# The expert loop of a mixture-of-experts tail: two expert numbers per register load, no runtime assert

## What is computed

```python
logits = jnp.einsum('bsh,eh->bse', x, router_w)
rw = jax.nn.softmax(logits, axis=-1).reshape(T, E)
vals, idx = jax.lax.top_k(rw, TOP_K)          # TOP_K = 2
w_masked = jnp.zeros_like(rw).at[jnp.arange(T)[:, None], idx].set(vals)
# out = sum over experts e of (x_flat * w_masked[:, e]) @ expert_weights[e]
x = x + out
```

## Time and profile before

| what | us |
|---|---|
| median of 3 executions | 2840.68 |
| lowest, highest | 2838.80, 2844.18 |
| profiled execution: span from first to last instruction | 2781.7 |
| median less span | 59.0 |

### The profile page before, as it was taken

One profiled execution on the slowest core, in us unless ns is written; L12 is line 12 of the kernel. 1 busy time (PEld: TensorE's weight loads), 2 busy tenths in 40 slices (PEclk: granted clock), 3 DMA queues, 4 the chain that ended last, 5 costly groups with the idle time before them and its releaser, 6 DMA issues. The chain is left out here.

```text
span 2781.7 us, 64142 instructions
## 1 busy us (share of the span) xinstructions
PE 2468.1 (89%) x25109; PEld 1445.1 (52%) x25113; DVE 1570.9 (56%) x2607; ACT 1793.8 (64%) x2682; POOL 737.1 (26%) x1006
## 2 busy tenths in 40 slices
PE   7888888887788989986999999999999998897982
PEld 4555655554667766653334333333344337676771
DVE  5767768577776457756554445555454437840223
ACT  3443535344455435546999999999999992465540
POOL 3203021030000017861211121211211120475566
PEclk9999999999899989988999999999999999899996
DMA  7810000000200004465766756666767605587887
GB/s 253 272 48 2 1 1 1 1 1 1 48 1 1 1 12 147 145 157 120 132 116 116 119 105 107 124 125 116 121 117 117 113 10 156 173 284 243 284 291 261
DMA packets 252048, 308.90 MB, mean 111 GB/s; under 512 B 100592, under 2 KB 180208, under 8 KB 251632
## 3 DMA queue, kind: packets, MB, share of 16 engines
q1 hardware_dynamic: 237392, 269.49, 41.2%
q0 software_dynamic: 12288, 33.57, 3.4%
q10 hardware_dynamic: 2080, 1.84, 0.2%
HBM read 157.23 MB, written 147.59 MB: 110 GB/s over the span
## 5 line engine op out<-in xcount | busy, mean ns | idle before, releaser
L1816 ACT ACTIVATE at_PT<-at_pS 128x1024 f32<-128x1024 f32 (+2 forms) x1152 | 1002.5, 1234 | 9.0 <-PE at_pS L1843 8.8
L1670 POOL TENSOR_SCALAR_AFFINE_SELECT at_PT<-at_PT 128x256 f32<-128x256 f32 (+1 forms) x384 | 197.4, 523 | 820.9 <-ACT at_PT L1816 820.5
L1843 PE MATMUL at_pS<-hd_QT,hd_KT 99*32 99x512 bf16 (+3 forms) x5120 | 317.1, 351 | 7.0 <-DVE at_QT L1788 5.0
L1843 PE MATMUL at_pS<-at_QT,at_KT 99*32 99x512 bf16 (+3 forms) x5120 | 318.9, 348 | 3.3 <-issue 1.3
L1767 DVE COPY md_y<-at_pO 128x512 f32<-128x512 f32 x64 | 44.2, 691 | 475.2 <-PE at_pO L1861 470.2
L1861 PE MATMUL at_pO<-at_PT,at_V 128*32 128x512 f32 (+3 forms) x2560 | 291.6, 529 | 0.6 <-POOL at_PT L1670 0.3
L1861 PE MATMUL at_pO<-at_PT,hd_V 128*32 128x512 f32 (+3 forms) x2560 | 287.0, 529 | 0.8 <-issue 0.8
L1843 PEld LDWEIGHTS at_pS<-hd_QT,hd_KT 99*32 99x32 bf16 x5120 | 111.9, 95 | 267.0 <-ACT at_PT L1816 173.2
L1843 PEld LDWEIGHTS at_pS<-at_QT,at_KT 99*32 99x32 bf16 x5120 | 118.2, 95 | 254.0 <-ACT at_PT L1816 161.8
L457 ACT ACTIVATE la_ft<-la_ft 128x1024 f32<-128x1024 f32 x128 | 135.2, 1056 | 160.8 <-DVE la_ft L280 160.5
L2423 PE MATMUL tl_bank<-tl_W,tl_xT 128*128 x884 | 224.5, 392 | 14.2 <-issue 12.8
(11 more groups left out here) (376 smaller groups left out, 4300.3 us busy)
## 6 DMA issues: line engine op xcount, KB each, us to landing
tl_xin<-rows_in SPq DMA_DIRECT2D x56, 512.0 KB, 5.4
score_terms<-at_parts SPq DMA_DIRECT2D x60, 384.0 KB, 5.8
rows_in<-la_zeros SPq DMA_DIRECT2D x8, 2048.0 KB, 7.9
rotated_qk<-qk_qkT SPq DMA_DIRECT2D x16, 1024.0 KB, 4.5
at_qk<-rotated_qk SPq DMA_DIRECT2D x60, 256.0 KB, 4.4
rows_out<-md_y SPq DMA_DIRECT2D x28, 512.0 KB, 3.7
rows_out<-tl_yout SPq DMA_DIRECT2D x28, 512.0 KB, 3.7
rows_in<-la_zeros SPq DMA_DIRECT2D x4, 3072.0 KB, 11.5
```

What stands on the lines that cost most here:

```text
L1670: nc.gpsimd.affine_select(out=d, in_=d, compare_op=ALU.is_ge, fill=0.0, base=0, pattern=of, channel_multiplier=-1).then_inc(masked, 1)
L1816: nc.scalar.activation(PT[u % 6][:, 0:banks, 0:width], pS[u % 3][:, 0:banks, 0:width], ACT.Exp, scale=HD ** -0.5).then_inc(exp_done, 1)
L1843: last = mm(pS[u % 3][r:r + 32, b, col:col + 512 - off], KT[par][0:KS, h, kb * P + r:kb * P + r + 32], QT[par][0:KS, h, c * 512 + off:(c + ...
```

## The change

Both numbers of a pair are fetched by one call, and the check that a number lies between 0 and 31 is left out of the program.

```diff
                 if j >= 3:
                     pe.wait_ge(y_ready, j - 2)
-                for w in range(blocks_of(j)):
-                    e = pe.value_load(which[0:1, 2 * j + w:2 * j + w + 1], min_val=0, max_val=E1 - 1)
+                blocks = blocks_of(j)
+                _, experts = nc.values_load_multi_w_load_instructions(
+                    which[0:1, 2 * j:2 * j + blocks], engines=[mybir.EngineType.PE], min_val=0, max_val=E1 - 1,
+                    skip_runtime_bounds_check_because="a count of experts, not negative, after a minimum with the last expert's number")
+                for w, e in enumerate(experts):
                     for a in range(DC):
                         last = mm(pP[j % 3][:, w * D:(w + 1) * D].unsqueeze(1), xT[(NP + j) % 4][:, w, a, :], W[:, a, ds(e, 1), :], start=(a == 0), stop=(a == DC - 1))
                 last.then_inc(multiplied, 1)
```

## The result

| | before | changed |
|---|---|---|
| median, us | 2842.12 | 2835.66 |
| executions | 20 | 20 |
| lowest to highest, us | 2834.24 to 2847.82 | 2827.83 to 2841.61 |
| ratio, 95% interval | | 0.9978, 0.9970 to 0.9986 |

The account below looks back on a forecast made before the run. TensorE's register fetches and a four-pair wait circle were taken to bound pairs 30 to 79. 2.34 against 2.48 us a pair gives 49 x 0.14 = 7 us, so 2840.7 - 7.0 = 2833.7 us, range 2828 to 2840.

Parts of the forecast that it names:

- stretch (b): Pairs 30 to 79, 2525.61 to 2647.30 us: only its shortening moves the end, 49 x 0.14 = 7 us.
- (c): Pairs 80 to 111: POOL's gathers run without a hole and cover TensorE, so nothing comes back there.
- The 59.0 us lie before the first and behind the last instruction: Step taking the 59.0 us between profiled span and measured time as lying outside the instructions.
- The circle: Pairs 30 to 79: copy, load, landing, fetch, products repeat every four pairs; 9.50 us before, 9.04 after.
- The remaining load brings two numbers: 0.05 us: Register load ahead of each pair: the second number adds 0.05 us, between bounds of 0 and 0.31.
- The assert goes: 0.31 us a block: Ahead of each block: register operation, assert and two steps between instructions vanish, saving 0.31 us.
- The slow load between blocks: Second load of each pair goes: saves 0.30 + 0.07 us a pair, up to 1.5 us where slow.
- Data in time: Rival, chance 0.14: landings get no later, 12 of the 15.4 us go, 2828.7 us.
- The transfers give it back: Rival, chance 0.16: loads land 0.4 us later with a faster TensorE, leaving 2 us gain, 2838.7 us.
- The loads were hidden anyway: Rival, chance 0.06: the queue before the array holds enough work, time stays at 2840.7 us.
- It doesn't do what it says: Rival, chance 0.05: the call becomes two loads or the 0.151 us operation stays; 2836.7 us.
- Slower: Rival, chance 0.05: each number is its own round trip; break-even at 0.51 us more per load, 2848 us.

Follow-up runs that it names:

- c3: Kernel before with fixed expert numbers, so no fetch, in pairs 0 to 29 and 80 to 111: 2832.22 us, ratio 0.9978 to before.
- c2: Changed kernel with the unchecked load of both numbers done twice ahead of every pair: 2844.91 us, ratio 1.0021 to the kernel before.
- b3: Changed kernel with both checks left in, one load for both numbers: 2839.57 us, ratio 1.0003 to the kernel before.
- b1_before_again: The kernel before, run and profiled again without an edit: 2837.66 us, ratio 0.9995.
- b2: Kernel before with the check left out, still two single loads per pair: 2831.99 us, ratio 0.9971 to before.
- b4: Fixed expert numbers in all pairs, no register load, check or register operation: 2825.53 us, ratio 0.9953 to the kernel before.
- d4: Fetch moved ahead, one unchecked load of four numbers for every two pairs: 2826.67 us, ratio 0.9954 to the kernel before.

## Why the prediction was right, and where not

*The size, 7 us, came out as 6.3.* The change does what it says, and it is faster by what was forecast. But this agreement is partly luck, since two steps were wrong and the count of circles moved.

*"The end moves by what stretch (b) gets shorter, and by nothing else" failed.* It rested on POOL's gathers running without a hole through (c) and TensorE's long rest ahead of pair 30. Both are true of the execution in the rows and of none that was profiled afterwards. c3 gained 6.2 us outside the middle. In its place: TensorE's last store sets the start of the last 32 gathers, and all 112 pairs, 28 circles, lie on that path.

*"The 59.0 us lie before the first and behind the last instruction" failed.* They were the difference between two kinds of execution. The timed spans show 1.8 us around them.

*The circle* held as a mechanism in its main point: a fetch behind a landing costs time in front of the products. c2 shows the dose: one more load, of 0.54 us at its shortest, costs 0.45 us a circle. Its arithmetic is not confirmed. The landing, 5.1 of its 9.50 us, comes from the short execution, and the timed kind shows none. And b3 agrees with the circle only by the numbers that it was expected with (0.31 longer by the second check, 0.2 shorter between blocks). These leave out the second number. With it, at 0.23 to 0.40 us, the circle would be 0.34 to 0.51 us longer, and the time 9.5 to 14 us in 28 circles; measured were 0.9 us, at the most 4.0 by the interval. Its trace has 51.3 us of waits ahead of products, 56.4 in b1_before_again, so it shows no longer circle either. Why both checks ahead of the first product cost so little stays open.

*"The remaining load brings two numbers: 0.05 us"* was mis-sized: 0.23 us where it is least disturbed, 0.36 to 0.40 in the mean, above the upper bound of 0.31. The value that the Trainium skill's page "Runtime: NRT & Kernel Launch" gives, about 200 ns for each register, stands in its section "Instruction fetch mechanics" (not in the one that the prediction names) and is for loads from HBM, which no run here makes. For two numbers from SBUF the trace comes near it (0.23 at the least disturbed), for four it doesn't (a median of 0.572 and a least of 0.329, where three more registers on 0.31 would make 0.9).

*"The assert goes: 0.31 us a block"* fits: b2 shows the check's part to be all of the gain that is seen, and 0.31 us in 28 circles is 8.7 us against 8.2 measured. The prediction's sum gave it the larger part too (0.31 of the 0.46 us that the circle was to lose, and 0.62 of the sequencer's 0.9).

*The slow load between blocks* as a part of its own isn't seen: b2 keeps it and loses nothing.

*The sum.* By the steps as measured, the circle loses 0.31 us by the check and 0.20 by the closed gap, and gains 0.23 to 0.40 by the second number. That leaves 0.11 to 0.28 us, in 28 circles 3.1 to 7.8 us (an estimate); the prediction had 0.46 in 12.25, 5.6, and some for the sequencer. More circles and a dearer load nearly cancel.

*The rivals.* "Data in time", 12 us, falls with the 6.3; even no fetch in any pair gave 13.3. "The transfers give it back" is half true, in another form: what comes back does so ahead of the transposes, in waits for issue and for ACT as much as for landings. "The loads were hidden anyway" falls with b2 and b4; the queue of 64 in the Trainium skill's "Advanced Engine Details and Errata", "Engine Queue Depths", doesn't hide them. "It doesn't do what it says" falls with the 112 loads. "Slower" would have needed 0.51 us more for a load; it was less. c2 passes that point, and is slower.

*What would show it.* In the changed kernel's own stretch (b), 2555 to 2682 us, the waits ahead of the products are:

```profile
PEld tl_bank L2426 <- issue: 9.9, 18, 1.5
PEld tl_bank L2372 <- DMA tl_xin<-rows_in: 8.4, 8, 1.8
```

In b1_before_again (2551 to 2678 us) it was 16.3 us in 37 waits. So the fall is of the kind forecast, but to 9.9 us and not to under 6, and the transposes do wait for `xin` several times. TensorE's longer rest ahead of pair 30, the first gather near 2645.5 and POOL's unbroken gathers, all named as signs, were absent. Two of the signs of being wrong came. The scatters of the second group ended at 2540 us in the changed kernel and at 2535 in b1_before_again, not near 2518. And the 64 gathers of group 1 start 1.50 us apart on average (94.3 us for 63 steps), not 1.27: POOL waits between them, 10.3 us of it for TensorE.

## What to carry to other kernels

Before a trace is taken for the measured kernel, compare its span with the times: here 59 us of difference were no overhead but a sign that the profiled execution was another kind, in which another engine decided the end. In this loop a register load and its check cost where they stand behind a wait for data, in the engine's own order. Leaving the check out gained, and so did fetching ahead of the wait without it. Fetching two numbers in one did not; the likely reason, that it puts the second number's time in front of the first product, is argued from the load's length. What was taken out of one wait in this circle of engines came back in part at another: look at the waits ahead of the other instructions of that engine before counting the whole.

## What the runs showed of the hardware that wasn't expected

A register load from SBUF took 0.307 us for one number (median of 221 in b2), 0.540 for two (median of 28 in the changed kernel's last stretch; 0.684 over all its 112), and for four 0.572 with a least of 0.329 (56 in d4, three of them of three numbers). Why four cost less per number than two was not tried.

In the long executions ACT waits without a releaser in the trace. In b1_before_again it waited 27.5 + 21.1 us for nothing visible ahead of its copies of products, and 26.8 ahead of those of transposed rows; the same view of the execution in the earlier trace rows has none of these waits:

```profile
ACT tl_yout L2296 <- remote: 27.5, 5, 12.0
...
ACT tl_xT L2289 <- remote: 26.8, 7, 9.9
...
ACT md_y L2296 <- remote: 21.1, 4, 10.7
```

They lie in the expert loop of all twelve experiments and of the changed kernel, with single holes of up to 16 us. The first two in b1, 6.90 and 6.42 us, are at places where ACT's program waits only for TensorE, which had been done for long; so they are no wait for a store. What ACT waits for there, and why one profiled execution had nothing of it, stays open. No experiment was made on it.
